# Reordering the value projections and regrouping one batch's router logits in a gated cross-attention + MoE kernel

## The reference, cut to what matters

```python
x = x + tanh(g_xattn) * attn(layernorm(x), ctx, ctx, mask)   # x (2, 512, 256), ctx (2, 1024, 256)
x = x + tanh(g_ffn) * ffn(layernorm(x))
# attn: q = x@Wq, k = ctx@Wk, v = ctx@Wv, 16 heads of 64; softmax with masked keys at -max; @Wo + bo
# ffn:  logits = xf@Wg + bg; idx = argmax(softmax(logits)); 8 experts, H = I = 256
#       y_e = gelu(xf@W1[e] + b1[e])@W2[e] + b2[e]; each token takes the one of its expert
```

## Time and profile before

| | |
|---|---|
| device time, median of 3 runs | 200.22 us (200.02 to 200.35) |
| device time of the profiled execution | 200.14 us |
| its span, first to last instruction | 198.3 us |
| PE busy | 185.5 us (94%) |
| DVE busy | 123.5 us (62%) |
| ACT busy | 104.9 us (53%) |
| POOL busy | 89.5 us (45%) |
| granted TensorE clock, mean | 0.99 |

### The profile page before, as it was taken

The page is one execution under the profiler, slowest core; times in us unless marked ns, Lnnn a source line. Parts: engine busy times, 40 slices in busy tenths (PEclk is TensorE's granted clock), DMA queues, the critical chain, the costliest instruction groups (busy, mean ns, idle before and its releaser), DMA issues.

```text
span 198.3 us, 4265 instructions
## 1 busy us (share of the span) xinstructions
PE 185.5 (94%) x1412; PEld 136.2 (69%) x1412; DVE 123.5 (62%) x538; ACT 104.9 (53%) x376; POOL 89.5 (45%) x128
## 2 busy tenths in 40 slices
PE   7999999999899999999999899998999999999960
PEld 6994455666665444788895666765788899989940
DVE  3479576899996421154459999997833556355520
ACT  3243438899998112211427899997631263445410
POOL 6000002577778991000003899768810024776650
PEclk9999999999999999999999999999999999999996
DMA  4998008999999990480000101600000002353011
GB/s 134 335 369 284 0 3 265 319 287 315 298 317 266 206 326 20 146 279 1 0 2 3 55 27 54 198 0 0 3 0 2 0 3 76 110 153 109 34 53 31
DMA packets 22323, 25.19 MB, mean 127 GB/s; under 512 B 1987, under 2 KB 20877, under 8 KB 22160
## 3 DMA queue, kind: packets, MB, share of 16 engines
q1 hardware_dynamic: 19536, 21.83, 37.3%
q0 software_dynamic: 1152, 2.12, 3.2%
q10 hardware_dynamic: 1600, 0.84, 1.5%
HBM read 14.14 MB, written 11.68 MB: 130 GB/s over the span
## 4 chain that ended last, share of the span: by engine, by line
PE 69%; DVE 21%; issue 3%; ACT 2%; POOL 1%; POOLq 1%; DVEq 0%
PE s_bank L1729 14%; PE o_bank L1674 14%; DVE probs L1308 12%; PE s_bank L2035 8%; PE o_bank L2046 7%; PE s_bank L1769 5%; DVE oT L1335 4%; PE s_bank L1608 3%; PE s_bank L1639 2%; PE o_bank L1817 2%; PE o_bank L1799 2%; PE t_bank L1700 2%; PE s_bank L1844 2%; ACT probs L832 2%; PE s_bank L2024 1%
## 5 line engine op out<-in xcount | busy, mean ns | idle before, releaser
L649 POOL TENSOR_TENSOR probs<-probs,r_col 128x512 f32<-128x512 f32 x32 | 33.3, 1040 | 73.8 <-DVE r_col L1319 73.7
L832 ACT ACTIVATE probs<-probs,negm_run 128x160 f32<-128x160 f32 x128 | 53.0, 415 | 6.1 <-DVE negm_run L1308 5.9
L1308 DVE CUSTOM_DVE_ANT_0 probs<-s_bank,maskneg 128x160 f32<-128x160 f32 x128 | 33.3, 317 | 3.5 <-PE s_bank L1769 3.2
L1729 PE MATMUL s_bank<-xnT,wq_sb 128*128 128x512 f32 x64 | 29.0, 600 | 0.0
L1674 PE MATMUL o_bank<-wo_sb,oT 128*128 128x256 f32 x128 | 28.7, 380 | 0.0
L1674 PEld LDWEIGHTS o_bank<-wo_sb,oT 128*128 128x128 f32 x128 | 23.9, 190 | 3.5 <-issue 0.5
L832 ACT ACTIVATION_READ_ACCUMULATOR probs<-probs,negm_run 128x1 f32 x128 | 23.9, 187 | 0.0
L1769 PE MATMUL s_bank<-k_sb,q_sb 64*128 64x160 f32 x256 | 21.7, 306 | 0.0
L1729 PEld LDWEIGHTS s_bank<-xnT,wq_sb 128*128 128x128 f32 x64 | 11.7, 190 | 13.1 <-issue 12.8
L628 POOL DMA_INDIRECT out_dram<-oT x16 | 17.0, 1064 | 7.8 <-DVE oT L1256 5.9
L1769 PEld LDWEIGHTS s_bank<-k_sb,q_sb 64*128 64x128 f32 x256 | 18.0, 187 | 2.7 <-DVE negm_run L1308 1.5
(11 more groups left out here) (169 smaller groups left out, 299.6 us busy)
## 6 DMA issues: line engine op xcount, KB each, us to landing
sorted_rows<-empty_row SPq DMA_DIRECT2D x8, 1040.0 KB, 15.6
oT<-in_L_ffn_W_dram SPq DMA_DIRECT2D x1, 2048.0 KB, 18.2
q_sb<-in_L_ffn_W_dram SPq DMA_DIRECT2D x1, 2048.0 KB, 9.4
oT<-sorted_rows SPq DMA_DIRECT2D x1, 1040.0 KB, 5.2
oT<-sorted_rows SPq DMA_DIRECT2D x8, 130.0 KB, 2.3
wq_sb<-in_L_xattn_Wq_dram SPq DMA_DIRECT2D x2, 512.0 KB, 8.1
mask_sb<-in_mask_BxSxS_bk_dram SPq DMA_DIRECT2D x2, 512.0 KB, 8.9
wv_sb<-in_L_xattn_Wv_dram SPq DMA_DIRECT2D x1, 1024.0 KB, 10.8
```

The costliest lines, as they stand in the source:

```text
L649: nc.gpsimd.tensor_tensor(window_wide(u), window_wide(u), r.rearrange("p i h -> p (i h)") .unsqueeze(2).broadcast_to([P, 4, WIDE]), ALU.mu ...
L832: last = nc.scalar.activation(window_part(u, i, h), window_part(u, i, h), ACT.Exp, bias=negm_run[at], scale=-1.0, accum_out=l_run[at])
L1308: nc.vector.tensor_tensor_reduce(window_part(u, i, h), s_bank[u % 2][:, h, i * CK:i * CK + WK], maskneg[:, q, 0:WK], -SCALE, LARGEST, ALU. ...
L1729: last = nc.tensor.matmul(bank[m % 4], wq_sb[:, c, m * P:(m + 1) * P], xnT[:, c, b * N:(b + 1) * N], start=(c == 0), stop=(c == DC - 1))
```

## The change

1. In `attend_window` PE's order becomes V0, `scores(2)`, left V, `scores(3)`, V1, and `take_left_v` waits for the second `v_ps` of the batch, not the third. DVE's becomes (after the maxima of unit 2) `take_left_v`, maxima of unit 3, copy of V1. Both batches take this order.
2. Batch 0's logits are no longer made tile by tile but in one call behind k2: the stationary operand is `wg_sb`, padded with zeros to 32 columns (`LEFT_E`), the moving one a 128-column token tile, and the four tiles go to the four column groups of the array, so that their result lies transposed, 32 partitions a tile. The bias product is 8 instructions, the rest 16. DVE copies the 128x128 result to SBUF (`take_logitT`), and PE transposes it back (`batch_logits_back`, behind k3) for `route_logits(0)`. Transpose 3 moves from behind k2 to behind k1.
3. POOL clears the padded `wg_sb` and `bg_sb` at the start; the ACT queue waits for that before it loads them, and the SP queue's wait for the empty row counts two more. Batch 1's logits stay as they were.

```diff
-        wg_sb = sb("wg_sb", [P, DC, E])
-        bg_sb = sb("bg_sb", [P, E])
+        wg_sb = sb("wg_sb", [P, DC, LEFT_E])
+        bg_sb = sb("bg_sb", [P, LEFT_E])
+        logitT = sb("logitT", [P, P])
...
-                sp.wait_ge(empty_ready, 2)
+                sp.wait_ge(empty_ready, 4)
...
+            nc.gpsimd.memset(wg_sb[:], 0.0).then_inc(empty_ready, 1)
+            nc.gpsimd.memset(bg_sb[:], 0.0).then_inc(empty_ready, 1)
...
+            act.wait_ge(empty_ready, 2)
+            act.dma_start(bg_sb[:, 0:E], bg.unsqueeze(0).broadcast_to([P, E])).then_inc(s_small, 16)
+            act.dma_start(wg_sb[:, :, 0:E], wg.rearrange("(c p) e -> p c e", p=P)).then_inc(s_small, 16)
...
+            def take_logitT():
+                dve.wait_ge(logit_ps, 1)
+                nc.vector.tensor_copy(logitT[:], bank[5][:, P:2 * P]).then_inc(logitT_taken, 1)
...
-                dve.wait_ge(first.v_ps, b * 3 + 2)
+                take_left_v(b)
+                window_max(b, 3)
+                dve.wait_ge(first.v_ps, b * 3 + 3)
                 nc.vector.tensor_copy(*window_v_dst(1)).then_inc(first.v_dve, 1)
-                window_max(b, 3)
-                take_left_v(b)
...
                 if where == "k1":
+                    take_logitT()
                     route_logits(0)
...
+            def batch_logits():
+                pe.wait_ge(xt2_sb, QT)
+                by_tile = [bank[5][t * LEFT_E:(t + 1) * LEFT_E, P:2 * P] for t in range(QT)]
+                for t in range(QT):
+                    nc.tensor.matmul(by_tile[t], bg_sb[0:1, :], ones[0:1, :], start=True, stop=False)
+                for c in range(DC):
+                    for t in range(QT):
+                        last = nc.tensor.matmul(by_tile[t], wg_sb[:, c, :], xnT[:, c, t * P:(t + 1) * P], start=False,
+                                                stop=(c == DC - 1))
+                last.then_inc(logit_ps, 1)
+            def batch_logits_back():
+                pe.wait_ge(logitT_taken, 1)
+                nc.tensor.transpose(bank[5][:, 2 * P:3 * P], logitT[:], ident[:]).then_inc(logit_ps, 1)
...
                 scores(2)
-                project_v(1)
-                also("v1")
-                scores(3)
                 if b > 0:
                     pe.wait_ge(first.k_dve, (b - 1) * 2 + 2)
                 project_v(2)
+                scores(3)
+                project_v(1)
+                also("v1")
...
                 if where == "k1":
-                    tile_logits(2)
+                    xn2_transposes(3)
                 elif where == "k2":
-                    xn2_transposes(3)
+                    batch_logits()
                 elif where == "k3":
-                    tile_logits(3)
+                    batch_logits_back()
...
                         project_tile(2)
-                        tile_logits(0)
                         xn2_transposes(1)
                         project_tile(3)
...
-                        tile_logits(1)
                         xn2_transposes(2)
```

More of the change, by code:

```diff
@@ L131, in flamingo_kernel @@
     NOWHERE = T
+    LEFT_E = P // QT
     sorted_rows = nc.dram_tensor("sorted_rows", [E * CH * P, RW], F32, kind="Internal").ap()
@@ L314, in flamingo_kernel @@
         logit_ps = sem("logit_ps")
+        logitT_taken = sem("logitT_taken")
         count_ready = sem("count_ready")
@@ L783, in _ @@
             act.dma_start(bo_sb[:], bo.unsqueeze(0).broadcast_to([P, D])).then_inc(s_small, 16)
-            act.dma_start(bg_sb[:], bg.unsqueeze(0).broadcast_to([P, E])).then_inc(s_small, 16)
-            act.dma_start(wg_sb[:], wg.rearrange("(c p) e -> p c e", p=P)).then_inc(s_small, 16)
+            act.wait_ge(empty_ready, 2)
+            act.dma_start(bg_sb[:, 0:E], bg.unsqueeze(0).broadcast_to([P, E])).then_inc(s_small, 16)
+            act.dma_start(wg_sb[:, :, 0:E], wg.rearrange("(c p) e -> p c e", p=P)).then_inc(s_small, 16)
             done = act.alloc_register("act_done")
@@ L1155, in route_logits @@
                 shape = [P, tiles, E]
-                logits = bank[5][:, at * E:(at + tiles) * E].rearrange("p (t e) -> p t e", e=E)
-                dve.wait_ge(logit_ps, r + 1)
+                if r == 0:
+                    logits = bank[5][:, 2 * P:3 * P].rearrange("p (t e) -> p t e", e=LEFT_E)[:, :, 0:E]
+                else:
+                    logits = bank[5][:, at * E:(at + tiles) * E].rearrange("p (t e) -> p t e", e=E)
+                dve.wait_ge(logit_ps, r + 2)
                 then(nc.vector.tensor_reduce(R.lmax[:], logits, AX.X, ALU.max))
@@ L1338, in take_left_v @@
             def take_left_v(b):
-                dve.wait_ge(first.v_ps, b * 3 + 3)
+                dve.wait_ge(first.v_ps, b * 3 + 2)
                 for h in range(2):
@@ L1400, in attend @@
                     nc.vector.tensor_copy(*k_dst(u + 1)).then_inc(S.k_dve, 1)
+                    also(f"k{u}")
                 dve.wait_ge(S.mask_ready, n + 1)
@@ L1442, in route_first_batch @@
             def route_first_batch(where):
-                if where == "k":
+                if where == "k1":
+                    take_logitT()
+                elif where == "k":
                     route_logits(0)
@@ L1696, in tile_logits @@
                         nc.tensor.matmul(bank[5][:, q * E:(q + tiles) * E].rearrange("p (t e) -> p t e", e=E),
-                                         ones[0:1, :], bg_sb[0:1, :].unsqueeze(1).broadcast_to([1, tiles, E]),
+                                         ones[0:1, :], bg_sb[0:1, 0:E].unsqueeze(1).broadcast_to([1, tiles, E]),
                                          start=True, stop=False)
                 for c in range(DC):
-                    last = nc.tensor.matmul(bank[5][:, at], xnT[:, c, tt * P:(tt + 1) * P], wg_sb[:, c, :], start=False,
+                    last = nc.tensor.matmul(bank[5][:, at], xnT[:, c, tt * P:(tt + 1) * P], wg_sb[:, c, 0:E], start=False,
                                             stop=(tt in LAST_ROUTED and c == DC - 1))
```

## The result

| | before | changed |
|---|---|---|
| median of 5 runs | 200.02 us (199.8 to 200.35) | 199.06 us (198.7 to 199.2) |
| ratio, 95% interval | | 0.995 (0.9926 to 0.9975) |
| span of the profiled execution | 198.3 us | 197.4 us |
| PE busy, PEld busy | 185.5, 136.2 us | 183.4, 132.8 us |

A forecast was written before the change was run, and what follows sets the result against it. PE bounds up to batch 1's first maximum, then DVE. Order of V -0.22, logits removed -1.77, batched logits +1.35, transpose back +0.13 sum to -0.51 us: 199.7 us from 200.22, range 199.2 to 200.5.

The forecast's parts named there:

- What bounds: PE between the attentions, then DVE alone from batch 1's first maximum to the left V copy's end; the tail only shifts.
- Order of V: Starts of both attentions: left transposes 0.22 us sooner in batch 0, nothing gained or lost in batch 1.
- Logits, removed: PE ahead of batch 1's attention: per-tile bias and logits taken out, 0.87 + 0.06 + 0.84, -1.77 us.
- Logits, added: Batched logits behind k2: 24 instructions at 0.033 us plus idle entry and exit, +1.35 us; bounds 0.95 and 1.70.
- the outcome of -0.3: Batched logits: if bias and main products count as two tiling modes, a drain between them leaves about -0.3 us in all.
- Sum: Whole kernel: -0.22 - 1.77 + 1.35 + 0.13 = -0.51 us; with the batched logits' bounds, -0.91 to -0.16.
- (a): Batch 1's head: just-met waits or a drain in the batched logits eat the gain, 199.9 to 200.2 us; chance 0.23.
- just-met wait: Batch 1's head: PE needs ACT's copy behind the table load and transpose 3's normalised tile just in time; no cost.
- a sign of being wrong: Batch 1's head: PE waiting more than 0.1 us for ACT's copy of transpose 3 would show the forecast wrong.
- (b): Batched logits: column groups do not overlap, so they cost +2.9 instead of 1.35, giving 201.2 us; chance 0.07.
- (c): Attention starts: left V's copies collide with POOL's normalisation, sum about +0.2, 200.4 us; chance 0.07.
- (d): Batch 1's head: batched logits near 1.0 and K parts without logits between them at 1.09, giving 199.2 us; chance 0.08.

The follow-up runs named there:

- v_order_only: Kernel before with only the new order of V, both batches, logits as before: 199.37 us against 199.99, ratio 0.9982.
- v_order_batch0: Changed kernel with the new order of V in batch 0 alone, batch 1 in the old order: 199.04 us against 199.99, ratio 0.9947.
- main_twice_grouped: Changed kernel with the 16 main instructions of the batched logits made once more ahead of the bias, in four column groups, into spare columns: 201.95 us, one execution.
- after_again: The changed kernel, unaltered, measured once more beside later follow-ups: 198.93 us, ratio 0.995.
- xt2_first: Changed kernel with ACT copying transpose 3 ahead of k1: 0.36 us under the changed kernel's repeat; tile 0 to batch 1's first maximum unchanged at 22.69 us.
- three doubled kernels: Changed kernel with main products doubled in four groups, main products doubled in one group, or bias and main products doubled: 201.95, 203.74, 202.48 us.
- twice_grouped: Changed kernel with bias and main products of the batched logits both made twice, in groups, extras first into spare columns: 202.48 us, one execution.

## Why the prediction was right or wrong

**What bounds.** Right: PE up to batch 1's first maximum, DVE from there (c is 8.28 to 8.29 in every kernel), and everything behind shifts as a whole (d 31.04 to 31.06).

**Order of V.** Batch 0: forecast -0.22, measured -0.22 (stretch a of `v_order_only`). Batch 1: forecast nothing, measured nothing (`v_order_batch0`).

**Logits, removed.** Forecast 1.77. From tile 0 to the context's first transpose it was 15.18 us (80.31 to 95.49) and is 14.26 (79.96 to 94.22): 0.92 for 0.87. From there to k1 1.53 and now 1.49: 0.04 for the 0.06, with the forecast wait for ACT. Logits 2 and 3 overlap with the K parts behind them, and no run removes them alone; with the forecast's 0.84 for them 1.80 was removed.

**Logits, added: the step that failed** is "24 x 0.033 = 0.79; the entry 0.17; the exit between 0.22 ... and 0.41 ... I take **+1.35**". From k1 to the scores it was 5.58 us and is 5.97. Taking off 0.84 and the 0.11 of the transpose back (100.39 to 100.50; 0.13 forecast), the batched logits cost 5.97 - 5.58 + 0.84 - 0.11 = 1.12 us, not 1.35. The weight loads say nearly the same without the 0.84: from the end of k2's loads (96.98 + 1.12 = 98.10) to the start of k3's at 99.19 it is 1.09. Term by term: 0.17 idle at the entry, as forecast; 0.15 + 0.38 = 0.53 of loading for the 0.79; 0.20 idle at the exit for the 0.22 to 0.41; and 0.20 idle between bias and main products, which the forecast had only as a risk.

The mechanism was right, the size was not, and the largest error is the pace: 0.033 us from one weight load to the next was read off left V's 16 instructions and multiplied by a number of instructions. Those have 256 moving columns. With 128 the pace is 0.018 (`main_twice_grouped`), so it went by columns rather than by instructions. No run changes the columns alone, but lengths from start to start agree: left V 1.00 for 16 instructions of 256 columns, the main products 0.57 for 16 of 128, the bias 0.35 for 8 of 128. If a bias instruction costs what a main one does, these give an estimate of (0.57 - 0.35) / 8 = 0.027 for an instruction of 128 columns, 0.13 around each group, and then (1.00 - 0.13) / 16 = 0.054 for one of 256. The 0.027 is about a quarter of the 0.104 that one group alone needs. It is more than the 0.018 between weight loads: part of what the products cost stands in the idle time behind the loads, so the loads' pace alone isn't a price.

The drain between bias and main products is there: 0.20 idle in every profile that has the two side by side. The Trainium skill, TensorEngine Tiling (Array Packing), Key Properties, says that changing the tiling mode drains the engine; the trace agrees. It is within the 1.12, so it did not bring the outcome of -0.3.

**Sum.** -0.22 - 1.80 + 1.12 + 0.11 = -0.79 us, inside the forecast's own bounds (-0.91 to -0.16) but 0.28 from its middle. That is the effect that the stretches show (0.22 in a, 0.57 in b). The measured 0.96 is 0.17 more. This is less than its interval, but `after_again` (1.07) and `v_order_batch0` (0.95) lie above 0.79 too, and only the ends of the run, which scatter by more, could hold it: whether some of it is real stays open. The range missed by 0.14 for three reasons together: it was counted from 200.22, whereas the median of before over five runs is 200.02 (from there it would have reached to 199.0); the batched logits were priced 0.23 too high; and these 0.17, which nothing explains. From the stretches alone one would get 200.02 - 0.79 = 199.23.

**Rivals.** (a) The waits were met as computed. Counted with the start's 0.15, ACT's copies of transposes 2 and 3 and of k1 begin within 0.02 of the forecast (95.50, 97.80 and 97.49 for 95.65, 97.96 and 97.63). Neither just-met wait cost anything: `xt2_first` shows it for ACT's copy, and the weight load of transpose 3 follows k1's loads without idle time. The 0.17 that the profile puts down to ACT's copy is over the 0.1 that the prediction named as a sign of being wrong, but moving the copy away left it as it was. (b) Refuted; in one group the main products add 1.85, near the 2.0 of the forecast, and 1.28 more than in four. (c) Refuted by the changed profile: 0.84 us for left V's two copies beside POOL. (d), more gained with cheap batched logits, is the direction in which it went: they cost 1.12, between the forecast's 1.35 and the 1.0 of (d). Its 199.2 was too low for its own terms: with 1.0 the sum is -0.86, and the K parts without logits between them were already in the 0.84 but for 0.04, which makes 199.3.

## What to carry to other kernels

A price taken from a neighbour in the trace must be scaled by what paces it, and taken from start to start, with the idle time behind it. Here 16 instructions of half the columns in the same four groups took 0.57 us where the neighbour's took 1.00, and counting instructions overpriced them. Small reorderings are better judged by the lengths between fixed marks (0.03 us of scatter) than by the run's time (0.4 us). Where the removal of cover opens a wait, look for independent work to put into it: the bias products cost 0.35 us behind k2 and 0.06 in front of k1. An idle bracket names who came last, not who cost the time: only moving ACT's copy away showed that its 0.17 was the change of shape.

## What the runs showed of the hardware that was not expected

The pace of column-group products: 16 instructions of 128 columns lengthen the stretch by 0.57 us in four groups and by 1.85 in one, each with a change of shape included. Each change of shape next to the batched logits shows 0.17 to 0.20 us of idle weight loading.

The ends of a run scatter more than its middle: the first scores start between 28.32 and 29.95 us. The eight filling products ahead of the first K part, here in before and in the changed kernel, tell the profiles apart:

```profile
5.59 2.08 PE L1608 MATMUL s_bank<-ones 128*128 128x128 f32 x8
```

```profile
5.45 1.16 PE L1626 MATMUL s_bank<-ones 128*128 128x128 f32 x8
```

In seven of the thirteen profiles they run for 2.08 us, and the first scores start at 29.49 to 29.95; in the other six for 1.16 or 1.17, and they start at 28.32 to 29.38. The changed kernel is on both sides (1.16 in its first profile, 2.08 in `after_again`), so the code doesn't decide it. The granted clock reads 1.00 in both stretches, and nothing here shows what does. In the changed kernel's first profile PE then waits 1.11 for a weight DMA ahead of the second K part, so that it reaches the first scores only 0.15 sooner than before.

In the three doubled kernels stretch e is 57.49 to 58.08 us, where ten others have 55.1 to 55.6. PE, DVE, ACT and POOL do the same as before up to the last store's issue (192.52 + 1.06 in `main_twice_grouped`, 191.77 + 1.07 in the changed kernel, at spans of 200.2 and 197.4); the surplus lies behind that, in the end of the last stores. In `twice_grouped` the time is moreover 3.1 us above the span, where it is 1.6 to 1.8 in the other profiles. The three ran together on one chip, but the one run of before beside them has a span of 197.3, so it wasn't there in every execution; whether the code or chance brings it stays open.
